# Second-layer recurrence four cycles later, and the first tiles' key copies, maxima and exponentials reordered, in a hand-scheduled attention and recurrence kernel

## What is computed

```python
# branch s: gated linear recurrence
xc = causal_conv(xn)                       # four taps, per channel
r, i = sigmoid(xc @ Wr.T + br), sigmoid(xc @ Wi.T + bi)
a = sigmoid(log_a) ** (8 * r)
h[t] = a[t] * h[t-1] + sqrt(1 - a[t]**2) * i[t] * xc[t]
s = rms_norm(h @ Wout.T) * gamma
# branch g: two layers of
q, k, v = shift(x) @ wqkv                  # 8 heads of 64
q, k = rotary(l2norm(q) * qs, l2norm(k) * ks)
x = x + softmax(mask(q @ k.T)) @ v @ wo    # blocks of 64, each with the one before
x = x + (a * gelu(g)) @ w2 + b2            # a, g = layer_norm(shift(x)) @ w1 + b1
out = x0 + s * silu(g_branch)
```

## The kernel before

| step | engine, line | what | first |
|---|---|---|---|
| rec_decay | ACT L580 | B <- exp(B), the decay a | -4 |
| rec_a2 | POOL L1263 | side <- B * B | -3 |
| rec_root | DVE L1063 | side <- max-clip of it | -2 |
| rec_root2 | ACT L585, L587 | side <- ln, exp: the square root | 1 |
| rec_input | POOL L1263 | A <- A * side | 2 |
| rec_scan | DVE L1068 | A <- scan of B, A | 3 |
| rec_out | PE | 4 matmuls on wr and A, bank 2 | 6 |
| rec_gamma, rec_square | DVE L1078, ACT L593 | read bank 2 | 6 |
| rec_sum | DVE L1072 | sum of squares | 8 |

## Time and profile before

### The profile page before, as it was taken

The page is one execution under the profiler, slowest core; times in us unless marked ns, Lnnn a source line. Parts: engine busy times, 40 slices in busy tenths (PEclk is TensorE's granted clock), DMA queues, the critical chain, the costliest instruction groups (busy, mean ns, idle before and its releaser), DMA issues.

```text
span 1305.3 us, 38178 instructions
## 1 busy us (share of the span) xinstructions
PE 1258.8 (96%) x13794; PEld 1006.3 (77%) x13794; DVE 1090.7 (84%) x1883; ACT 1162.4 (89%) x3529; POOL 1145.7 (88%) x840
## 2 busy tenths in 40 slices
PE   7999999999999999899978999999999999999998
PEld 4778888888888887566656788888888888876776
DVE  6888888888888886699878898989889998883777
ACT  5889999999999998887768899999999999998886
POOL 4999999999999987499779999999999999984776
PEclk9999999999999999999999999999999999999999
DMA  5222222222222211011011122122122221110223
GB/s 168 54 63 63 62 62 63 63 66 73 63 71 71 56 41 35 17 35 36 1 30 36 41 53 47 46 47 46 46 48 54 54 46 46 38 39 25 70 76 97
DMA packets 60298, 70.04 MB, mean 54 GB/s; under 512 B 8912, under 2 KB 38288, under 8 KB 60112
## 3 DMA queue, kind: packets, MB, share of 16 engines
q1 hardware_dynamic: 60112, 67.61, 20.8%
HBM read 13.33 MB, written 4.19 MB: 13 GB/s over the span
## 4 chain that ended last, share of the span: by engine, by line
PE 75%; POOL 10%; DVE 5%; ACT 4%; issue 4%; DMA 1%; SPq 0%; DVEq 0%; ACTq 0%; POOLq 0%
PE ps L203 59%; PE ps L268 8%; POOL t L1263 4%; PE ps L278 3%; PE ps L281 3%; POOL hxr L1263 2%; ACT P L657 2%; POOL P L1263 1%; DVE t L979 1%; POOL side L1293 1%; DVE t L991 1%; DVE nm L1010 1%; DMA B<-in_wqkv 0%; ACT sqk L631 0%; PE ps L445 0%
## 5 line engine op out<-in xcount | busy, mean ns | idle before, releaser
L657 ACT ACTIVATE P<-ps,nm 128x128 f32<-128x128 f32 x1024 | 364.4, 385 | 2.3 <-DVE nm L1010 1.9
L203 PE MATMUL ps<-wqkv,hT 128*128 128x512 f32 x1152 | 329.2, 427 | 15.5 <-DVE t L979 11.8
L1263 POOL TENSOR_TENSOR t<-t 128x1024 f32<-128x1024 f32 x128 | 307.5, 2403 | 34.4 <-DVE t L979 31.7
L1263 POOL TENSOR_TENSOR P<-P,rden 128x512 f32<-128x512 f32 x256 | 292.4, 1152 | 23.5 <-DVE rden L1017 21.6
L203 PEld LDWEIGHTS ps<-wqkv,hT 128*128 128x128 f32 x1152 | 214.5, 188 | 94.9 <-issue 28.2
L1263 POOL TENSOR_TENSOR t<-t,rr 128x1024 f32<-128x1024 f32 x128 | 244.2, 1908 | 18.6 <-ACT rr L640 18.4
L657 ACT ACTIVATION_READ_ACCUMULATOR P<-ps,nm 128x1 f32 x1024 | 230.6, 225 | 0.0
L991 DVE TENSOR_TENSOR t<-ps,tabl 128x512 f32<-128x512 f32 x256 | 164.2, 682 | 41.2 <-ACT sqk L631 39.7
L1263 POOL TENSOR_TENSOR hxr<-hxf,hxr 128x512 fp32r<-128x512 f32 (+1 forms) x93 | 131.0, 1437 | 67.0 <-ACT hxr L713 67.0
L1010 DVE TENSOR_REDUCE nm<-ps 128x4 f32<-128x512 f32 x256 | 173.4, 679 | 5.2 <-PE ps L203 5.1
L647 ACT ACTIVATE PT<-ps 128x1024 f32<-128x1024 f32 x128 | 130.6, 1020 | 51.1 <-PE ps L268 50.0
(11 more groups left out here) (140 smaller groups left out, 2544.1 us busy)
## 6 DMA issues: line engine op xcount, KB each, us to landing
Vs<-Vn SPq DMA_DIRECT2D x224, 128.0 KB, 2.4
side<-in_x SPq DMA_DIRECT2D x17, 256.0 KB, 3.0
A<-X SPq DMA_DIRECT2D x16, 256.0 KB, 2.5
norm<-X SPq DMA_DIRECT2D x32, 128.0 KB, 2.2
norm<-X SPq DMA_DIRECT2D x32, 127.8 KB, 2.4
hsh<-X SPq DMA_DIRECT2D x31, 128.0 KB, 2.3
hsh<-X SPq DMA_DIRECT2D x31, 127.8 KB, 2.3
oT<-in_x SPq DMA_DIRECT2D x15, 256.0 KB, 3.0
```

Source lines behind the costliest of these rows:

```text
L203: return e.matmul(o, lhsT, rhs, start=start, stop=stop, skip_group_check=True)
L657: k = act(P[:, g, :], ps[:, 3 + s, (g % 4) * 128:(g % 4 + 1) * 128], ACT.Exp, bias=nm[:, g:g + 1], accum_out=den[:, g:g + 1])
L1263: return e.tensor_tensor(o, a, b_, op)
```

## The change

**The recurrence of layer 2** is put four cycles later: the firsts above become 0, 1, 2, 5, 6, 7, 10, 10 and 12 (rec_out at 10). Sequences 0 and 1 need no ramp entries any more. At the other end the last sequences get some: rec_root2(15) in cycle 63, rec_input(15) in cycle 64, rec_scan(15) in cycle 65, rec_out, rec_gamma and rec_square of sequence 14 in cycle 65 and of sequence 15 in cycle 66, rec_sum(14) in cycle 66 and rec_sum(15) in cycle 67. PE's waits for bank 2 follow.

**In both layers** `exps(0, 0)` is issued in cycle 2 ahead of `square(2)`, where it was the cycle's last operation on ACT, and `keep_k(1)` in cycle 2 behind `rotate(2)`, where it was in cycle 3.

**In layer 2** besides: `keep_k(0)` stands between the parts of `rotate(1)`; both `row_max` of tile 0 stand ahead of `norm_sum(1)`; `gates2(15)` moves from the end of layer 1's MLP phase to cycle 2 behind `norm_sum(2)`; the copies of w1 and w2 on ACT go from cycles 5 and 6 to 2 and 4, and their low parts on DVE from cycles 6 and 7 to 3 and 5.

The diff, cut to its core:

```diff
             e.wait_ge(s_rv, l * NB + b + 1)
-        elif l and (b := hit(i, 6)) is not None:
-            e.wait_ge(s_osq, b + 1)
...
             extra = False
-            if l and (b := hit(i, 6)) is not None:
-                side_free(l, i - 1)
-                rec_out(b, 2)
-                extra = True
+            if l:
+                for b in due(i, 10, {NB - 2: -1, NB - 1: NT + 2}):
+                    side_free(l, i - 1)
+                    rec_out(b, 2)
+                    extra = True
...
                 ln_turn(b, 2)
+                extra = True
+            if l and i == NT + 1:
+                side_free(l, i - 1)
+                rec_out(NB - 2, 2)
...
                         e.wait_ge(s_x, hit(i, -4) + 1)
+                elif i == NT + 1:
+                    e.wait_ge(s_osq, NB - 1)
+                elif i == NT + 2:
+                    e.wait_ge(s_osq, NB)
                 elif hit(i, 10) is not None:
-                    e.wait_ge(s_osq, hit(i, 6) + 1)
+                    e.wait_ge(s_osq, hit(i, 10) + 1)
...
             e.wait_ge(s_wo, 2 * (m - 1) + t // 2 + 1)
+        elif l and t == 0:
+            e.wait_ge(s_xi, NB)
...
                 ln_root(1)
+            if i == 2:
+                exps(l, 0, 0)
...
             else:
-                for b in due(i, -4, {0: 1, 1: 3}):
+                for b in due(i, 0, {}):
...
                     root_var(l, b)
-                for b in due(i, 1, {0: 4, 1: 6}):
+                for b in due(i, 5, {NB - 1: NT - 1}):
...
                     square_hc(l, b)
-                if (b := hit(i, 6)) is not None:
+                for b in due(i, 10, {NB - 2: NT + 1, NB - 1: NT + 2}):
...
                 norm_rt(l, 1)
-            if i == 5:
+            if i == (2 if l else 5):
...
                 act(w1r[:, 0, :], w1, ACT.Copy, scale=lcol(l, 0)).then_inc(s_whi, 1)
-            if i == 6:
+            if i == (4 if l else 6):
...
                 keep_p(l, i - 3)
-            if 0 <= i - 2 < NT:
+            if 0 < i - 2 < NT:
...
                     scale_hc(l, b)
-                for b in due(i, -2, {0: -1, 1: 5}):
+                for b in due(i, 2, {}):
                     rec_root(b)
-            if 0 < i - 2 < NT:
+            if 1 < i - 2 < NT:
...
             else:
-                if (b := hit(i, 8)) is not None:
+                for b in due(i, 12, {NB - 2: NT + 2, NB - 1: -1}):
...
                     centre(l, b, 2)
-                if (b := hit(i, 6)) is not None:
+                for b in due(i, 10, {NB - 2: NT + 1, NB - 1: NT + 2}):
                     rec_gamma(b, 2)
-                for b in due(i, 3, {0: 5, 1: 8}):
+                for b in due(i, 7, {NB - 1: NT + 1}):
...
                 proj_add(l, b, 0, 2)
-            if i == 1:
+            if i == 1 and l:
+                row_max(l, 0, 0)
+                row_max(l, 0, 1)
+            elif i == 1:
                 keep_k(l, 0)
+            if i == 2:
+                keep_k(l, 1)
...
                 norm_sum(l, i)
-            if i == 1:
+            if i == 1 and not l:
...
                 row_max(l, 0, 1)
+            if l and i == 2:
+                gates2(NB - 1)
...
                 ln_stats(1)
-            if l and i == 3:
-                rec_root(0)
...
                 set_decay(i - NT - 1)
-            if i == 6:
+            if i == (3 if l else 6):
...
                                        ALU.mult, ALU.subtract).then_inc(s_wlo, 1)
-            if i == 7:
+            if i == (5 if l else 7):
...
                     down_add(0, NB - 1)
-                    for p in range(3):
+                    for p in range(2):
                         rotate(1, 1, p)
+                    keep_k(1, 0)
+                    rotate(1, 1, 2)
...
                 down_add(l, b - 1)
-            if l == 0 and b < NB:
+            if l == 0 and b < NB - 1:
...
                 normalise(l, i - 3, 0)
-            for b in due(i, 2, {0: 5, 1: 7}) if l else ():
+            for b in due(i, 6, {NB - 1: NT}) if l else ():
...
                     shift_hi(l, b)
-                for b in due(i, -3, {0: -1, 1: 4}):
+                for b in due(i, 1, {}):
...
                 add_qk(l, i)
-            if l and i == 2:
-                rec_a2(0)
```

## The result

| | before | changed |
|---|---|---|
| median of the runs (lowest to highest) | 1309.04 us (1307.43 to 1315.69, 11 runs) | 1315.76 us (1312.07 to 1318.98, 11 runs) |
| ratio, changed to before | | 1.0039, 95% interval 1.0026 to 1.0052 |
| profiled execution, own time; span | 1307.07; 1305.3 us | 1316.67; 1314.9 us |
| granted clock in it | 0.999 | 0.991 |

What follows compares the result with a forecast made beforehand. PE, busy 96% of the span, was taken as the bound. Start -2.5, end +3.75 and layer 1 +0.6 made +1.85 us: 1308.9 for the profiled execution, 1310.5 us as median, range 1303.5 to 1315.0.

Steps and rivals of the forecast that it cites:

- the prediction's own band of 0.3%: Whole kernel: differences within about 0.3%, 3.9 us, count as no change; the band is 1304.7 to 1312.6 us.
- Middle of layer 2, nothing: Layer 2, cycles 12 to 62: same instructions in the same places for the sequence before, cost 0.
- Tile 0 later: Start of layer 2: tile 0's scaling waits for rec_decay(0), its transposes come 2.7 us later, tiles 2 and 3 4.6 to 5.0.
- What goes: Start of layer 2, behind tile 3: compressed steps of sequences 0 and 1 vanish, 5.8 us on DVE, 3.8 counted.
- The term of -2.5 for the start: Start of layer 2: net gain of 2.5 us from tile 0's delay and the removed steps, bounds -6.2 and 0.
- The bound of 0: Start of layer 2: no net gain if the contention of DVE and POOL merely lands elsewhere.
- The end, +3.75: End of layer 2: rec_root2(15) and rec_out(14) make tile 63's similarities 3.75 us later, bounds 0 and +5.0.
- the delay reaches the end: End of layer 2: last attention and MLP hang on tile 63, so its +3.75 us carries through to the end.
- Layer 1, +0.6: Layer 1: exps(0,0) ahead of square(2) costs 0.6 us, bounds 0 and +1.5; keep_k(1) costs 0.
- Rival 3: Layer 1: four scale_hc flips between long and short, 4 us either way: 1306.5 or 1314.5 us; chance 0.12.
- Rival 2: Start of layer 2: late start not won back as contended DVE operations move, +4.9 us in all, 1313.6; chance 0.18.
- Rival 1: Layer 2: start wins 6.2 us, end mostly absorbed at +1.25; total -4.35, 1304.3 us; chance 0.20.

Runs made afterwards that it cites:

- the repeat: The changed kernel itself, unaltered, measured again on chip 9 against the kernel before: ratio 1.0040 (1.0022 to 1.0058).
- the shift alone: The kernel before with only layer 2's recurrence four cycles later, start order as before: ratio 1.0008 (0.9994 to 1.0021) to before.
- the shift with rec_out in 64: The kernel before with the recurrence four cycles later and rec_out(14) in cycle 64, not 65: 0.9967 of before, repeated on another chip 0.9988.
- the key copy back: The changed kernel with keys and maxima of tile 0 in their old places, decay and square of sequence 0 still early: 1.0012 of before.
- layer 1 as before: The changed kernel without its two layer 1 edits (exponentials of tile 0, key copy of tile 1): ratio to before 1.0028 (1.0015 to 1.0042).
- end rearranged: The changed kernel with rec_out(14) behind tile 63's similarities and rec_root2(15) behind cycle 63's exponentials: ratio to before 1.0040 (1.0024 to 1.0055).
- the filler: The changed kernel with unread matmuls added in idle PE time, 9 before tile 0's transposes, 7 before rec_out(14): 1.0014 of before, clock 0.994.

## Why the prediction was right and wrong

- **The number**: 1314.1 us by the ratio lies 0.9 us inside the stated range, the median 0.8 us outside. By the prediction's own band of 0.3% the ratio of 1.0039 is slower, which had a chance of 0.22, and not the same, which had 0.54. Start and end were both forecast too well, by 1.8 and 1.4 us, and layer 1's chance lengths could as well have added more; that the range held is partly luck.
- **Middle of layer 2, nothing**: right, 401.67 against 401.70 us from tile 12 to 63.
- **Tile 0 later**: right by mechanism and nearly by size. Transposes +2.56 us (2.7 forecast), rotate(1)'s last part +3.5 (3.7). norm_sum(1) is 5.1 late where I had 4.0, square(2) 5.8 where I had 4.6: the 1.1 us between is row_max waiting 1.53 us for products at the low clock. Tile 3 came 6.05 us late, not 4.6 to 5.0.
- **What goes**: right, -6.70 us from tile 3 to 10 where the working had -7.0. The long rec_root and rec_scan of the earlier trace rows are gone, though tile 5, behind the later tile 3, comes at 43.14 us and not at the 41.85 forecast (41.39 before). The forecast's 704.2 doesn't follow from its own terms: 4.6 to 5.0 us late less 3.8 makes 704.5 to 704.9.
- **The term of -2.5 for the start** was so the first mis-sized one: -0.65 us to tile 10, -0.77 to tile 12 (repeat: -1.45, -1.56). The bound of 0 held it. The working had two things wrong. The removed steps are worth 4.7 us by themselves (the shift alone), not the 7 to 8.3 of the working; of the 6.70 above some 2 us are tile 3's delay made up again. And tile 3's delay is 6.05 us and not up to 5.0, of which 1.1 stand under the low clock; the contention that the bound was meant for wasn't there.
- **The end, +3.75**: right to the similarities and the first w1 matmul (+3.55 each). rec_root2(15) gave +1.2, the wait for centre(14) and what is behind it 2.4. But +5.12 us came in all. **The step that failed** is "the delay reaches the end" as the only consequence of a wait, which costs idle PE by its length alone: in the repeat the clock fell right behind the wait, made the 32 products 1.73 us long and put the first w1 matmul 1.56 us later still. In the first profile the remaining 1.6 us lie elsewhere: the clock was 0.84 between 1210 and 1220 us, some 37 us behind the wait. That stretch is low in the repeat of the shift with rec_out in 64 as well, which doesn't have this wait, so that it followed from the change isn't shown.
- **Layer 1, +0.6**: neither confirmed nor ruled out. Rival 3's idea was right, that scale_hc flips between long and short, but it happens from one execution to the next: either code varies by 4 to 6 us in its attention phase, where 5 to 12 of the 14 are long. In the first two profiles the flips cancelled (6 long in each). The MLP phase varies by 3.5 us, so the 5.25 us of the first profile are mostly chance. The MLP phase's lengths weren't in the forecast at all.
- **Rival 2** (slower) had about the number (1313.6), but by the wrong mechanism; the slow side of rival 3 (1314.5) was as near it, and its flips cancelled. rec_root(0) took 0.68 us in the changed kernel, the low part of w2 0.73. With the key copy back rec_root(0) did meet POOL (t<-t,rr there, until 685.66) and took 1.91. The Trainium skill's rule on the shared port (SBUF — State Buffer, Who interferes with whom) agrees with that row, but it wasn't what decided.
- **Rival 1** needed tile 10 at 77.7 us. No kernel had less than 78.98, so my -6.2 was out of reach in any case.

The ratio of 1.0039 is then made of: start about -1.2 us (mean of the two profiles to tile 12; -0.2 with the two further kernels that have this start, layer 1 as before and end rearranged), end +5.1 us, together 3.9 to 4.9, and perhaps something in layer 1. That is within 3.4 to 6.8. Of it, about 1 us at the start (the extra delay of norm_sum(1)) and 1.6 at the end stand in stretches with a low clock. Set against the shift alone, the start's reordering costs 3.1 of these microseconds.

## What to carry to other kernels

Cost a new wait of the engine that is the bottleneck twice: once by its length, once by what its clock may do behind it (1.1 to 2.9 us a time here), and check the granted clock of each stretch before explaining a difference. An operation for an early result (the first tile's key copy) placed inside the next tile's work ties two chains together; look for who waits behind it first. At the end of a loop, put leftover side work in the cycle in which its buffer is free, not the one in which its data first would be: moved by one cycle, it took the shifted kernel from 1.0008 of before to 0.9967 and, repeated, 0.9988.

## What the runs showed of the hardware

The granted clock tends to fall behind new waits of PE, which the forecast didn't have. All ten kernels with a reordered start have it at 1.2 GHz in some stretch between 673 and 700 us, none of the four with the old start (before, shift alone, and the shift with rec_out in 64 twice) has. In layer 1's MLP phase seven of the ten executions with the wait of 2 us have it low just behind, none of the four without the wait has. Five of the seven kernels in which PE waits 2.4 us for centre(14) and isn't given filler have it low from that wait on, the other two not there but some 37 us later. This is where the low stretches lie, not a test: the one experiment made to test it, the filler, didn't decide. In such stretches the q and k products of a tile took 1.73 to 1.92 us instead of 1.04 to 1.07, nine projection matmuls 4.19 instead of 2.35. The Trainium skill (TensorE: Matmul & The Clock Gate, Part 1: The HAM clock gate) says that a clock gate sets the array to one of two rates by how busy it has been; the traces agree, with 0.50 and 1.00 in the windows inside such stretches and outside. But stretches near 15 to 41 and 584 to 597 us are low in one execution and not in another of the same code (the shift with rec_out in 64 had none there the first time and two the second), so single executions of this kernel differ by several microseconds before any change is made. Executions of before ranged from 1305.4 to 1316.5 us; so a ratio here needs a dozen executions a side, and one profile shows places, not the size.
